# A first expert layer that computes only the chosen experts, block by block, in a four-layer kernel

## What is computed

```python
x = x + tanh(g_xattn[0]) * xattn0(layernorm(x), ...)          # long filter, stage A
x = x + tanh(g_ffn[0]) * ffn0(layernorm(x), ...)              # experts, stage B
x = x + tanh(g_xattn[1]) * xattn1(layernorm(x), ctx, ctx)     # attention, stage C
x = x + tanh(g_ffn[1]) * ffn1(layernorm(x), ...)              # shared matrices with adapters, stage D
# ffn0, E, K = 8, 2 ; F = 176 ; FS = 704
probs = softmax(x @ Wr)
routing_weights, selected = top_k(probs, K)
C = einsum('tk,tke->te', routing_weights, one_hot(selected, E))
expert_out = vmap(lambda wg, wu, wd: silu(x @ wg) * (x @ wu) @ wd)(Wg, Wu, Wd)
moe_out = einsum('te,eth->th', C, expert_out)
shared = sigmoid(x @ Wsg) * (silu(x @ Sg) * (x @ Su) @ Sd)
out = moe_out + shared
```

## Time and profile before

| | us |
|---|---|
| median of 3 runs | 888.54 |
| lowest and highest | 885.79 and 888.65 |
| the profiled execution | 884.61 |
| its span | 882.9 |
| stage A | 0 to 179.6 |
| stage B | 179.6 to 481.9 |
| stage C | 481.9 to about 618 |
| stage D | to the end |

### The profile page before, as it was taken

The page is one execution under the profiler, slowest core; times in us unless marked ns, Lnnn a source line. Parts: engine busy times, 40 slices in busy tenths (PEclk is TensorE's granted clock), DMA queues, the critical chain, the costliest instruction groups (busy, mean ns, idle before and its releaser), DMA issues.

```text
span 882.9 us, 13668 instructions
## 1 busy us (share of the span) xinstructions
PE 790.2 (90%) x4692; PEld 638.1 (72%) x4708; DVE 613.5 (69%) x1231; ACT 325.4 (37%) x521; POOL 163.9 (19%) x176
## 2 busy tenths in 40 slices
PE   3887879689999999999999899987789999999995
PEld 2565757578978888887887566655568787887884
DVE  5999999654465466446645888888377867778754
ACT  2120212033343342333233678765245335343221
POOL 1899989600000000000000112111000000000000
PEclk9999999799999999999999899997789999999997
DMA  7221212000000000000000121210101001001000
GB/s 274 73 81 56 71 48 66 18 1 1 1 1 0 0 0 0 0 0 27 25 0 15 40 85 56 86 48 1 49 0 49 1 25 49 1 25 49 24 1 24
DMA packets 21147, 30.24 MB, mean 34 GB/s; under 512 B 3760, under 2 KB 16112, under 8 KB 20464
## 3 DMA queue, kind: packets, MB, share of 16 engines
q1 hardware_dynamic: 21104, 29.69, 10.2%
HBM read 27.55 MB, written 2.13 MB: 34 GB/s over the span
## 4 chain that ended last, share of the span: by engine, by line
PE 67%; DVE 18%; issue 7%; POOL 3%; ACT 3%; DMA 1%; DVEq 0%; SPq 0%; POOLq 0%; ACTq 0%
PE bank L1630 23%; PE bank L1484 20%; PE bank L1497 11%; DVE small L1062 2%; PE bank L1551 2%; DVE A L868 2%; DVE A L857 2%; PE bank L1537 2%; POOL A L449 2%; DVE A L1072 2%; PE bank L1409 2%; ACT A L632 1%; PE bank L1411 1%; PE bank L1410 1%; PE bank L1562 1%
## 5 line engine op out<-in xcount | busy, mean ns | idle before, releaser
L1630 PE MATMUL bank<-R 128*128 128x512 f32 (+4 forms) x1104 | 225.9, 365 | 19.1 <-DVE A L1190 5.0
L1630 PEld LDWEIGHTS bank<-R 128*128 128x128 f32 (+2 forms) x1104 | 182.3, 188 | 60.1 <-issue 6.0
L1484 PE MATMUL bank<-R 128*128 128x512 f32 (+1 forms) x816 | 198.0, 392 | 1.9 <-issue 1.9
L1484 PEld LDWEIGHTS bank<-R 128*128 128x128 f32 (+1 forms) x816 | 146.7, 185 | 33.2 <-issue 2.1
L1009 DVE TENSOR_TENSOR A<-bank,A 128x512 f32<-128x512 f32 (+1 forms) x68 | 47.0, 691 | 119.9 <-PE bank L1484 119.9
L1497 PEld LDWEIGHTS bank<-R 128*128 128x128 f32 (+1 forms) x816 | 105.8, 190 | 10.8 <-issue 4.0
L574 ACT ACTIVATE A<-bank 128x512 f32<-128x512 f32 (+1 forms) x68 | 40.7, 599 | 194.6 <-PE bank L1484 194.6
L1497 PE MATMUL bank<-R 128*128 128x256 f32 (+1 forms) x816 | 109.4, 283 | 2.5 <-DVE R L1020 2.1
L1409 PE MATMUL bank<-A 128*128 128x256 f32 x128 | 45.4, 438 | 26.1 <-DVE A L857 17.6
L449 POOL TENSOR_TENSOR A<-A 128x256 f32<-128x256 f32 x64 | 64.3, 1004 | 12.4 <-DVE A L868 12.4
L1202 DVE TENSOR_TENSOR A<-bank,A 128x512 f32<-128x512 f32 (+1 forms) x48 | 32.9, 685 | 33.0 <-PE bank L1630 32.8
(11 more groups left out here) (166 smaller groups left out, 1105.2 us busy)
## 6 DMA issues: line engine op xcount, KB each, us to landing
A<-in_w SPq DMA_DIRECT2D x17, 384.0 KB, 3.1
A<-rows_d SPq DMA_DIRECT2D x4, 1024.0 KB, 4.7
A<-in_w SPq DMA_DIRECT2D x8, 480.0 KB, 3.5
A<-in_ctx_one SPq DMA_DIRECT2D x8, 272.0 KB, 3.5
A<-in_ctx_half SPq DMA_DIRECT2D x8, 256.0 KB, 3.1
A<-in_ctx_nat SPq DMA_DIRECT2D x4, 512.0 KB, 3.6
A<-in_ctx_t SPq DMA_DIRECT2D x128, 16.0 KB, 2.0
out<-X SPq DMA_DIRECT2D x4, 512.0 KB, 2.9
```

What stands on the lines that cost most here:

```text
L1484: mm = nc.tensor.matmul(dst[0:pr], wX[:, j, at + k * P:at + k * P + pr], mX[:, k], start=(n == 0), stop=(n == 5))
L1630: mm = nc.tensor.matmul(dst, a, m, start=start and n == 0, stop=stop and n == len(prods) - 1, skip_group_check=skip)
```

## The change

Stage B now computes the shared expert for all tokens, and the eight experts only for the rows that chose them.

- Routing gives every token two slots, one in each chosen expert's region of a table x_d in the chip's memory (18304 rows of 264 numbers: 256 of the normalised token and 8 weights). The rank of a token in its expert comes from matmuls with a triangle of ones (b_rank). Group 0 is routed as part 0, during stage A; the other twelve sequences are part 1, routed in one go beside the shared tiles of group 1.
- GpSimd scatters the rows: 32 indirect transfers of 128 rows, 8 for part 0 and 24 for part 1.
- A table of 39 blocks (NBLK, 32 full and up to 7 begun ones) says for each block where its 128 rows start and which expert it belongs to. SyncE, TensorE and VectorE load from it into registers (TENSOR_LOAD): one a block on SyncE, two on TensorE, one on VectorE.
- A block: SyncE loads 128 rows, TensorE turns them (2 matmuls), 6 matmuls of 352 columns give gate and up with tokens in the partitions, 2 turn the hidden part, 6 of 256 columns give down; ScalarE rounds twice and takes SiLU, VectorE subtracts twice, multiplies, and scales the result by the token's weight into yo; SyncE stores it to y_d. Four steps of different blocks are interleaved. Six row buffers (xb) and four result buffers (yo) are used in turn.
- GpSimd gathers: 32 indirect transfers with addition bring two rows of y_d back into X for each token.
- The order is: shared tiles of groups 0 and 1 (PRE = 2), the 39 blocks, shared tiles of groups 2 and 3. The last shared tile, 64 columns, now holds gate and up side by side, 6 matmuls in place of 12.
- The experts' weights are loaded (experts_in), rounded on ScalarE and subtracted on GpSimd in 10 chunks beside the first shared tiles. In stage A only the six shared tiles are split, 4 of them between heads; the inverse root there is one power on GpSimd (a_pow).
- Stage C takes over the statistics of groups 2 and 3 into its steps. Stage D packs its last tile in the same way (d_base_tail). Loops over groups are written out.

```diff
+NBLK = 2 * B + E - 1
...
+NCHUNK = 10
...
+SPLITS = {(0, 5): 2, (0, 10): 3, (1, 5): 4, (1, 10): 5}
...
+            for i in range(E - 1):
+                sp.dma_start(x_d[E * CAP + i * P:E * CAP + (i + 1) * P, :], zeros).then_inc(rows_zeroed, 16)
+            sp.wait_ge(table_ready, 1)
+            for i in range(E):
+                at = sp.value_load(tz[0:1, i:i + 1], min_val=0, max_val=E * CAP)
+                sp.dma_start(x_d[bass.ds(at, P), :], zeros).then_inc(rows_zeroed, 16)
+            sp.wait_ge(rows_zeroed, 16 * (2 * E - 1))
+            sp.wait_ge(rows_scattered, 16 * 2 * B)
+            def block_in(i):
+                if i < 6:
+                    if i < 4:
+                        sp.wait_ge(xsL_ready, NCHUNK)
+                else:
+                    sp.wait_ge(y_made, i - 5)
+                at = sp.value_load(trow[0:1, i:i + 1], min_val=0, max_val=X_ROWS - P)
+                sp.dma_start(xb[i % 6], x_d[bass.ds(at, P), :]).then_inc(blk_loaded[i % 6], 16)
+            def block_out(i):
+                sp.wait_ge(y_made, i + 1)
...
+            def a_pow(g):
+                pool.wait_ge(ve_ready, g + 1)
+                nc.gpsimd.tensor_tensor(rs[:], ve[:], mhalf, ALU.pow).then_inc(pow_ready, 1)
...
+                    if (g, h) in SPLITS:
+                        split_low(SPLITS[g, h])
...
+            def scatter(b):
+                for r in range(2):
+                    nc.gpsimd.indirect_dma_start(
+                        out=x_d[:, :], out_offset=bass.IndirectOffsetOnAxis(ap=slots[:, b, r:r + 1], axis=0),
+                        in_=row_of(b), in_offset=None).then_inc(rows_scattered, 16)
+            def gather(b, r):
+                nc.gpsimd.indirect_dma_start(
+                    out=X[:, b], out_offset=None, in_=y_d[:, :],
+                    in_offset=bass.IndirectOffsetOnAxis(ap=y_slots[:, b, r:r + 1], axis=0),
+                    compute_op=ALU.add).then_inc(gathered[r], 16)
...
+                pool.wait_ge(y_stored[i], 16 * ((NBLK - 1 - i) // 4 + 1))
+            pool.wait_ge(y_slots_ready, 2)
+            for g in range(G):
+                if g == PRE and PRE < G - 1:
+                    zero_keys()
+                pool.wait_ge(b_done, 1 + 2 * (g + 1))
+                for b in range(g * BG, (g + 1) * BG):
+                    gather(b, 0)
+                pool.wait_ge(gathered[0], 16 * BG * (g + 1))
+                for b in range(g * BG, (g + 1) * BG):
+                    gather(b, 1)
 
             def split_low1(g, r):
...
+            def blk_low_x(i):
+                dve.wait_ge(bxH_ready, i + 1)
+                nc.vector.tensor_tensor(bxL[:, i % 2], XT[i % 2][:, 0:D], bxH[:, i % 2].bitcast(F32), ALU.subtract
+                                        ).then_inc(bxL_ready, 1)
+            def blk_hidden(i):
+                dve.wait_ge(bsilu_ready, i + 1)
+                if i >= 2:
+                    dve.wait_ge(bh_turned, i - 1)
+                nc.vector.tensor_tensor(bh[:, i % 2, 0:EF], GU[i % 2][:, EF:2 * EF], bsilu[:, i % 2, 0:EF], ALU.mult
+                                        ).then_inc(bh_ready, 1)
+            def blk_low_h(i):
+                dve.wait_ge(bhH_ready, i + 1)
+                nc.vector.tensor_tensor(bhL[:, i % 2], HT[i % 2][:, 0:D], bhH[:, i % 2].bitcast(F32), ALU.subtract
+                                        ).then_inc(bhL_ready, 1)
+            def blk_out(i):
+                col = dve.value_load(tcol[0:1, i:i + 1], min_val=D, max_val=D + E - 1)
+                dve.wait_ge(bdown_ready, i + 1)
+                if i >= 4:
+                    dve.wait_ge(y_stored[i % 4], 16 * (i // 4))
+                nc.vector.tensor_scalar(yo[i % 4], DB[i % 2][:, 0:D], xb[i % 6][:, bass.ds(col, 1)], None, ALU.mult
+                                        ).then_inc(y_made, 1)
...
+            def blocks():
+                blk_low_x(0)
+                for s in range(NBLK + 2):
+                    if s + 1 < NBLK:
+                        blk_low_x(s + 1)
+                    if s < NBLK:
+                        blk_hidden(s)
+                    if s >= 2:
+                        blk_out(s - 2)
+                    if 1 <= s <= NBLK:
+                        blk_low_h(s - 1)
 
...
+                if g + 2 < G:
+                    dve.wait_ge(gathered[1], 16 * BG * (g + 3))
+                    norm = c_norm(BG * (g + 2), BG * (g + 3))
...
-                    pe.wait_ge(silu_ready, J0 * g + j - 1)
-                else:
-                    pe.wait_ge(h_ready, 1 + J0 * g)
-                for at, dst in ((0, G_[j % 2]), (2 * P, U_[j % 2])):
-                    if j >= 2 and at:
-                        pe.wait_ge(scaled_ready, J0 * g + j - 1)
-                    n = 0
...
+            def blk_gate_up(i):
+                at = pe.value_load(t16[0:1, i:i + 1], min_val=0, max_val=(E - 1) * RANK)
+                pe.wait_ge(bxL_ready, i + 1)
+                if i >= 2:
+                    pe.wait_ge(bh_ready, i - 1)
+                m = 0
+                for xX, wX in ((bxH, guH), (bxH, guL), (bxL, guH)):
+                    w = wX.rearrange("p (j a k c) -> p k a j c", j=EJ, a=2, k=DT)
+                    for k in range(DT):
+                        mm = nc.tensor.matmul(GU[i % 2][:, 0:2 * EF], xX[:, i % 2, k * P:(k + 1) * P],
+                                              w[:, k, :, :, bass.ds(at, RANK)], start=(m == 0), stop=(m == 5))
+                        m += 1
+                mm.then_inc(bgu_ready, 1)
...
+            def blk_down(i):
+                at = pe.value_load(t256[0:1, i:i + 1], min_val=0, max_val=(E - 1) * D)
+                pe.wait_ge(bhL_ready, i + 1)
+                if i >= 2:
+                    pe.wait_ge(y_made, i - 1)
+                m = 0
+                for hX, w0_, w1_ in ((bhH, dH0, dH1), (bhH, dL0, dL1), (bhL, dH0, dH1)):
+                    for rows, w in ((P, w0_), (EK, w1_)):
+                        a0 = 0 if w is w0_ else P
+                        mm = nc.tensor.matmul(DB[i % 2][:, 0:D], hX[0:rows, i % 2, a0:a0 + P],
+                                              w[0:rows, bass.ds(at, D)], start=(m == 0), stop=(m == 5))
+                        m += 1
+                mm.then_inc(bdown_ready, 1)
...
+            def blocks():
+                pe.wait_ge(table_ready, 1)
+                pe.wait_ge(h_ready, 1 + SJ * PRE)
+                pe.wait_ge(b_done, 1 + 2 * PRE)
+                blk_turn(0)
+                for s in range(NBLK + 1):
+                    if s + 1 < NBLK:
+                        blk_turn(s + 1)
+                    if s < NBLK:
+                        blk_gate_up(s)
+                    if s >= 2:
+                        blk_down(s - 2)
+                    if s >= 1:
+                        blk_turn_h(s - 1)
+                pe.wait_ge(bhL_ready, NBLK)
+                pe.wait_ge(bxL_ready, NBLK)
+                b_gate_up(SJ * PRE)
+                blk_down(NBLK - 1)
 
...
+            def d_base_tail(g):
+                j = SJ - 1
+                pe.wait_ge(tail_packed, 2)
+                dst = U_[j % 2]
+                three(dst, [(w1_tile(j, k * P, P), (xH[:, k], xL[:, k])) for k in range(DT)], stop=False, skip=True)
+                three(dst, [(w1_tile(j, 4 * P, P), (dzH[:, 0], dzL[:, 0]))], start=False, stop=False, skip=True)
+                return three(dst, [(w1_tile(j, 4 * P + TAIL, P), (dzH[:, 2], dzL[:, 2]))], start=False, skip=True)
...
+            for g in range(PRE):
+                b_group(g)
+                if g + 1 < PRE:
+                    b_gate_up(SJ * (g + 1))
+                    b_side(SJ * (g + 1))
+                b_down(SJ * g + SJ - 1)
+                if g + 1 < PRE:
+                    b_side_late(SJ * (g + 1))
+            blocks()
+            for g in range(PRE, G):
+                if g > PRE:
+                    b_gate_up(SJ * g)
+                b_group(g)
+                b_down(SJ * g + SJ - 1)
+            pe.wait_ge(h_ready, 1 + SJ * G)
...
```

940 lines of the change are left out of this document (638 added, 302 removed).

## The result

The changed kernel takes 946.0 us (median of 4 runs, 942.8 to 948.3) against 887.2 us for the kernel before on the same chip: a ratio of 1.066 with an interval of 1.062 to 1.070. It is slower; the forecast was 846 and its range ended at 895. The profiled execution took 942.8 us, its span is 941.1 (before: 884.6 and 882.9).

What follows compares the result with a forecast made beforehand. The prediction took TensorE, busy 90% of the span, to bound the kernel, with VectorE pacing part of stage A. From 884.6 us, -9 - 29.9 + 5 - 5.5 = -39.4 gave 845; it predicted 846, range 800 to 895.

Steps and rivals of the forecast that it cites:

- the ring: Stage B blocks: load of block i+5 issued only behind block i's store; 2T = 3.5 + 2.7, T = 3.1 us.
- T: Period of one block in stage B's loop; forecast 3.3 us, 39 blocks plus 4 for filling making 132.7 us.
- the rival of the prediction: Blocks: register loads stand in the open on TensorE, at 1.3 us each T = 4.7; 901 us, chance 0.13.
- the gap: Stage B ahead of the blocks: TensorE idle 31.3 us for 24 scatters, landings and first block; ends 17 and 50.
- The price of a down product: Blocks on TensorE: each 256-column down product takes 0.119 us, six of them within 2.11 us of work a block.
- The clock: Blocks: a granted clock of 0.77 at 73% busy lengthens 1.9 us of products; a reason for 3.3 over 3.1.
- The first two shared groups: Stage B ahead of the gap: 47.4 us of tiles, 60 with turnings, logits, edges and stalls; ends 55 and 72.
- The last two groups: Stage B behind the blocks: shared tiles with nothing beside them, 48.4 us with their end.
- Stage A: Before stage B: Newton steps and stalls beside GpSimd leave VectorE, routing adds 2 us; -9 us, ends -3 and -16.
- Stage C: Attention stage: takes over two groups' statistics, 4.5 us each on VectorE, half showing; +5 us, ends 0 and +9.
- The one on indirect transfers: Scatters and gathers: indirect transfers cost 2 us or more each, gap grows by 19; 879 us, chance 0.17.
- The faster one: Blocks run at TensorE's pace, register loads nearly free and landings short, T = 2.4; 811 us, chance 0.2.

Runs made afterwards that it cites:

- the first experiment: Changed kernel with each block's six down products issued as three of 128 rows, then three of 48, instead of alternating: 910.5 us, ratio 1.028.
- the ring and none: Changed kernel with each 48-row down product replaced by the 128-row one, leaving out part of the sum: 902.4 us, ratio 1.018.

## Experiments: what held the blocks

**Rows loaded one block sooner, on top of the order by rows.** Six row buffers were there; only the place in SyncE's queue held the load back.

```
-for i in range(4):
+for i in range(5):
     block_in(i)
 for i in range(NBLK):
-    if i + 4 < NBLK:
-        block_in(i + 4)
+    if i + 5 < NBLK:
+        block_in(i + 5)
     block_out(i)
```

> By rows as in the first experiment, and SyncE issues the load of block i+5 ahead of the store of block i, not behind it (five loads ahead of the loop, where there were four). Theory (with the row changes gone, the period of 3.4 to 3.6 us is the ring of store, load and landing that the prediction wrote down): TensorE's waits for a block's rows (35 us in the first experiment) go, the period at full clock falls to TensorE's own work and hand-overs, 2.8 to 3.0 us, and the clock stays over 0.9: 38 x (3.67 - 2.9) = 29 us less than 910.5, about 881 (875 to 888). Rival (the landing itself, or the register load ahead of the gate/up products, 0.41 us in the open, sets the period): 3.2 us or more, 893 to 910.

Measured: 876.2, T 2.77, 1.3% less than the kernel before (the interval ends at 0.994). By now it seemed that the ring mattered only once the changes of rows were gone, so the sooner load was also tried alone.

> The changed kernel with its alternating down products as they are, and only the row loads issued one block sooner. Theory (TensorE's own 3.56 us a block at full clock is later than the ring of loads, so the ring costs nothing here): 941 to 948, no change. Rival (part of the blocks' 4.31 us is the ring, through the half-clock stretches that its waits bring): 925 to 938.

Measured: 900.4. That theory fell: one line in SyncE's order is worth 46 us with every change of rows still there. The table by stretch:

```profile
300.00:350.00 50.00, 50.00 (x241) 36.83 (x241) 23.62 (x61) 14.65 (x45) 0.00 (x0) 1.00 0.27 79
350.00:395.00 45.00, 45.00 (x218) 33.03 (x217) 21.05 (x54) 12.70 (x39) 0.00 (x0) 1.00 0.27 81
```

TensorE is busy 50.0 of 50 with 241 matmuls, where the changed kernel was busy 47.1 with 176, and the clock is 1.00 instead of 0.80. The single periods are 3.33 at full clock (the 3.23 of the table has the three short ones in it): that is TensorE's own pace with six changes of rows.

**The ring shortened at its other end.** On TensorE the gate/up products of block s are put ahead of the turning of block s+1.

> The changed kernel, alternating rows and late loads as they are, with one pair of steps swapped on TensorE in the block loop: the gate/up products of block s stand ahead of the turning of block s+1, not behind it. Loading one block sooner took 46 us off (900) where no change was expected, so the old theory (TensorE's own 3.56 us are the limit) has fallen. New theory (the ring of store, load and landing holds the blocks; the turning that waits for the landing keeps the register steps and the six gate/up products behind it from starting, 1.7 us that stand in the ring): taken out of the ring, TensorE's own work of 3.33 us at full clock with the row changes becomes the limit and the clock stays up: 38 x (4.31 - 3.33) = 37 us less, 900 to 912. Rival (the sooner load helped for another reason, such as the spread of the DMA traffic over the period): 940 to 949.

Measured: 911.4, within the 900 to 912 of the theory. Most single periods are 3.32 to 3.39; T is 3.55, since some are longer, up to 4.86, with a mean clock of 0.95 over the blocks:

```profile
355.75 0.33 PE L2001 MATMUL bank<-ident,A 128*128 128x128 f32 x1
355.92 0.27 PE L2002 MATMUL bank<-ident,A 128*48 128x128 f32 x1
355.94 1.25 PE L1992 MATMUL bank<-R 128*128 x6
357.03 0.38 PE L1979 MATMUL bank<-ident,A 128*128 128x128 f32 x2
```

The loads are issued behind the stores as before, so the traffic is not it; the ring is.

**The ring in numbers.** In the changed kernel, from one store to the one two blocks on, 350.68 to 358.67, are 7.99 us, so 2T = 8.0 at full clock: 3.26 from the store to the turning (351.76 is its load, landed and turned at 353.94), 0.84 from the turning to the products, 1.29 to the down products, 1.87 for these, 0.73 to the next store. The 0.84 holds only 0.22 of turning. The rest are the register steps of the next products (a load of 0.30 us, arithmetic of 0.15, a check), which stand behind the wait in TensorE's program and so begin when it ends, the load at 353.93 like the turning itself: the [0.41 <-issue] above. One step earlier, where nothing was waited for, the same load ran at 349.5, beside the products before, and the gate/up products began 0.15 us behind the turning (350.22 and 350.37). The register steps of the down products make 1.29 of what is 1.08 with the loads one block sooner.

So the 4.51 from the fourth turning on are 3.33 of TensorE's own work, 0.67 that the ring adds (8.0/2), and 0.5 that are left, which goes with the stretches at half the clock: periods that fall into them take 5.6 to 6.0. The mean granted clock over the blocks was 0.80 with ring and changes of rows, 0.87 with the ring and two changes, 0.96 with the ring and none, 0.95 with all the changes and the products first, and 0.98 with all the changes and the loads sooner. So it takes both, waits for rows and stalls between products; how the two add up in the chip these runs do not settle.

**No register loads on TensorE.** All blocks take expert 1's weights at fixed addresses, in gate/up and down.

> The run with the early statistics (870), and TensorE loads no register in the blocks: all of them take expert 1's weights at fixed addresses. It prices the rival of the prediction in which the loads lie in the open. Theory (a load of 0.30 us runs ahead of the products of its step for the most part; between the last gate/up product and the first down product 0.1 to 0.3 us of it shows): 39 x 0.1 to 0.3 = 4 to 12 us less, 858 to 866. Rival (wholly hidden): 868 to 872. Rival of the prediction (0.65 us or more each in the open): 50 us less.

Measured: 857.6, 12.5 less than the 870.0 of the kernel with earlier statistics (below), with T 2.45 instead of 2.77: 0.32 us a block for two register loads and what belongs to them, a little over the 0.1 to 0.3 of the theory. It prices them where no rows are waited for; in the changed kernel the load of the gate/up products also stands in the ring, as above. From one block's products to the next's, 340.76 to 343.24:

```profile
340.76 1.24 PE L1991 MATMUL bank<-R 128*128 128x352 f32 x6
341.84 0.82 PE L2011 MATMUL bank<-R 128*128 128x256 f32 x4
...
343.24 1.24 PE L1991 MATMUL bank<-R 128*128 128x352 f32 x6
```

2.48 less two changes at 0.19 is 2.10; the forecast had 2.11 for the products and turnings alone. (No kernel was run that has neither.)

## Experiments: the shared groups around the blocks

**The first eight scatters behind the expert chunks.** They stand between chunk 1 and 2 on GpSimd, and ahead of the 11.78 us of idle at 211.11 ScalarE waits 8.19 us for a chunk's load, with the hidden tile's SiLU behind it.

> The eight scatters of the first four row groups are issued behind the ten expert chunks on GpSimd, not between chunk 1 and 2. Theory (the 12 us idle of TensorE before 211 in the first shared groups comes from the chunk loads that wait for GpSimd behind the scatters): the idle goes, the later scatters fit ahead of the second routing part, 8 to 13 us less, 946 -> 933 to 938. Rival (the chunk loads themselves, or SyncE's small transfers, end last anyway): 0 to 3 us less, 943 to 949.

Measured: 951.3, no gain, although the 11.78 us are gone: 3.79 are left there, and the longest wait in the two groups is 4.25. Tried again on the mended blocks:

> As the run before it, and the first eight scatters behind the expert chunks. Alone this gave nothing on the time (951 against 946) although the first turning of a block came 3.7 us sooner, because the blocks then ran at a lower clock. Theory (that came from the row changes, which are gone): 3 to 5 us less than the run before it, about 869. Rival (the lower clock in the blocks comes from the longer stretch at full clock ahead of them, whatever they do): no gain.

Measured: 873.3 against 870.0, no gain either. GpSimd's timeline tells why, with the scatters early (first row) and late:

```profile
249.42 1.31 POOL L626 DMA_INDIRECT x_d<-A  x1 [8.31 <-DVE A L1297]
```

```profile
251.35 0.96 POOL L626 DMA_INDIRECT x_d<-A  x1 [0.30 <-issue]
252.62 0.96 POOL L626 DMA_INDIRECT x_d<-A  x1 [0.30 <-issue]
```

Early, the ninth scatter waits for VectorE's slots, 78.2 us behind the first shared product (171.26); late, it has no wait for slots but stands behind the eight, at 76.6 (175.98). The eight cost 10 to 11 us wherever they stand on GpSimd. Something is gained: from the first shared product to the first turning of a block it is 112.1 us late, against 114.2 in the run that it is compared with; but that run's profile began its shared tiles 4.7 us sooner, with the same stage A, and a gain of 2 us does not show in times that spread by 6 to 9. My first reading of the missing gain, that the lower clock in the blocks (T 4.50) ate it, does not explain the second run, whose blocks are as fast as the others.

**The low parts of the experts' weights only cleared.** On the kernel with late scatters, GpSimd clears them and does not subtract, so they are left out.

> The run with early statistics and late scatters (873), with the ten subtractions on GpSimd that make the low parts of the experts' weights (L622, 2.4 us each) replaced by clearing the same memory, so the low parts are left out. It prices the expert chunks in the first two shared groups. Theory (GpSimd's subtractions stall VectorE's small steps by 2.2 us each, four or five times, and hold the next chunk's load): the stalls of 2.3 us on VectorE are gone, the first scatter of the second part comes 72 us or less behind the first gate/up product where it came 76.6, and the time is 3 to 7 us less, 866 to 870. Rival (the chain from the norms over the logits to the ranks sets it, whatever GpSimd does): 76 us, 871 to 876.

Measured: 863.0, 10 less and so below the 866 to 870 of the theory, the ninth scatter 70.6 us behind the first shared product instead of 76.6, the first turning 106.0 instead of 112.1. VectorE's stalls beside GpSimd are gone: three small steps had taken 2.42, 2.23 and 2.33 us (L1061, L1073, L1216), and now none does. One line of VectorE with its least, median and most in ns, first where GpSimd subtracts, then where it clears:

```profile
L1216 DVE TENSOR_TENSOR A<-A,ramp x2: 257/1294/2332, 239.0 to 243.1; 128x96 f32<-128x96 f32 x2
```

```profile
L1216 DVE TENSOR_TENSOR A<-A,ramp x2: 258/258/259, 233.3 to 235.3; 128x96 f32<-128x96 f32 x2
```

GpSimd itself also works 14 us less (0.9 us a chunk for 2.3), and its queue is what the ninth scatter stands in. But GpSimd is idle for ScalarE's rounding of the next chunk 52.5 us with the subtractions and 59.7 without, so it is one link of a chain (load, rounding, subtraction, buffer free), and no engine that works throughout. So with late scatters the chain of the chunks sets the length of these groups, and GpSimd's link is worth 6 us of it; the share of VectorE's stalls in these is not told apart.

**Statistics of the first group sooner.** VectorE's `c_norm(0, BG)` two tiles sooner, ScalarE's `c_norm_one` one.

> As the run before it, and VectorE's statistics of the first group for the attention (L1428) stand two tiles sooner, ScalarE's normalising (L815) one tile sooner; TensorE's turning of q stays where it was. Theory (the 8.6 us of TensorE idle ahead of the turning of q in the last shared group are this chain of 4.6 us of small steps and 2.1 us of normalising, put behind the last tile's work): the idle goes, 6 to 9 us less than the run before it, about 873. Rival (VectorE then waits two tiles sooner for the gathers, with the hidden tiles queued behind it): 0 to 3 us less, or more time.

Measured: 870.0 against 876.2; the intervals overlap (0.978 to 0.988, 0.980 to 0.994), so the times alone do not show a gain. The trace is plainer. The idle of 8.63 us ahead of the turning of q is now 2.91, and the last two groups take 58.5 us for 66.6:

```profile
451.49 1.97 PE L1966 MATMUL bank<-ident,A 128*128 128x128 f32 x8 [2.91 <-ACT A L737]
```

**Three shared groups ahead, one behind** (`PRE = 3`).

> The run with deeper loads (876), with three shared groups ahead of the blocks and one behind, where it has two and two. Theory (the 24 later scatters, 1.26 us each, hold the gap of 27.6 us, and a shared group beside them hides it; the gathers need about 22 us a group behind the blocks, and only one shared group of 24 us is left to hide them): the gap falls to under 10 us and the third group runs at full clock, -20 us; the last group's turning of q and the first scores wait for gathers, +5 to +15 us: 861 to 871. Rival (the gathers come late for the whole attention stage, since the 32 of the first two groups take 40 us): +20 to +40, 876 to 896.

Measured: 863.1, a ratio of 0.972 (0.969 to 0.975) to the kernel before: the best version here that computes everything. TensorE's timeline at both ends of the blocks:

```profile
290.93 0.66 PE L1979 MATMUL bank<-ident,A 128*128 128x128 f32 x2 [2.33 <-DMA A<-x_d]
...
440.95 1.97 PE L1966 MATMUL bank<-ident,A 128*128 128x128 f32 x8 [12.75 <-ACT A L737]
```

The third group lies wholly in the gap: the blocks start at 290.9, as they do with two groups ahead. What it buys is partly given back: the turning of q waits 12.75 us for the gathers, and stages C and D take 419.8 instead of the 402.7 of the kernel with two groups ahead (876.2).

## Why the prediction was wrong, step by step

- **The price of a down product failed.** "6 x 0.160 + 6 x 0.119 + 4 x 0.11 = 2.11 us" took the 0.119 of 256 columns from tiles whose products all have the same rows. The 0.160 was right (0.167), the turns were right, and 2.10 came out once the changes were taken off; but every one of the six products stands at a change of rows, 0.312 us. Four changes fewer take the period from 3.34 to 2.84 from the fourth turning on, 0.50 us and not 4 x 0.19 = 0.76: from the first gate/up product to the first down product it is now about 1.3 us where it was 1.08, since the register steps between them, which the changes had covered, now show.
- **The ring was the right mechanism, and its sizes failed.** "2T = load + 2.7" with a load of 3.5: the load was 3.26. For the turning I had 0.22 and it is 0.84, since the register steps stand behind its wait; for the products 0.96, and 1.29; for down 0.71, and 1.87; for the rest 0.8, and 0.73. 6.2 became 8.0. The text had all the pieces: it named the ring, said that "the rows of a block are fetched late" and that TensorE has two register loads a block, and then placed these beside the ring instead of in it.
- **The clock was seen and under-priced.** I allowed 0.2 us of T for it and for the register loads together, from a stretch at 0.77; it came at 0.80 and the period of 4.51 has 0.5 that nothing else accounts for. It came with the ring and the changes of rows together, and goes with either.
- **The first two shared groups failed by 29 us.** I named the right scene, a late chunk, SiLU behind it, TensorE behind that, and gave it under 3 us. The idle times above 0.5 us there sum to 21.4 (11.78, 1.95, 0.53, 2.09, 3.94, 1.08), and the clock falls to 0.68 in the stretch around the longest. Taking the longest away moved the start of the blocks, counted from the first shared product, by 2.4 us at most: the chain of the chunks with GpSimd's 23 us of subtractions and 10 of scatters holds it, or VectorE's routing, whichever ends later. How the rest of the 29 us divides was not measured.
- **The last two groups failed by 20 us.** "48.4 with their end" left out 6.7 us of statistics and normalising behind the last tile (8.63 of idle), of which 8.1 came back when they were put sooner (66.6 to 58.5), and a clock of 0.88 and lower (475 to 500 us, 0.84 after it); that the clock makes up the other 10 us is argued, not shown.
- **What held.** A scatter is issued every 1.26 us (1.2 forecast), and the gap is 27.6 (31.3), by luck in part: the ninth scatter comes 8.4 us ahead of the end of the second group, where 3.5 was forecast, and the 24 take a little longer. Stage A gained 4.7, inside its ends of -3 and -16; that varied from 171 to 176 us for the first shared product between kernels with the same stage A. Stage C, up to the first of stage D's three-part products, lost 7.3 (+5, ends 0 and 9), stage D gained 2.4 where I had 5.5. Neither of these stages' edits was tried alone.
- **The rivals.** The slower one (register loads in the open, T = 4.7, 901) is near in T and mostly wrong in cause: a load is 0.30 us and not 1.3, and two cost 0.32 us a block where nothing is waited for. It is right for the gate/up load where it stands behind a wait for rows: up to 0.69 us, in 13 of some 36 periods (295 to 455 us). The one on indirect transfers is refuted for scatters (every 1.26 us); the gathers, every 1.84, come near it, and what they cost was not tried. The faster one, T = 2.4, is near what the kernel could do: 2.77 was reached, and 2.45 without register loads. Of what the text said the profile would show, the gap came as written, the pace did not, and the waits ahead of the products were of both kinds it named, for rows and "issue", one behind the other.

## What to carry to other kernels

Before pricing a matmul by its columns, look whether its neighbour has the same count of rows; write products of one row count in a row. In a loop of transfers and work, put the whole ring on paper from the rows, register steps behind a waiting instruction included, and ask which engine's program order holds a step that its data would allow: two edits of order, worth 70 us together, turned a kernel 6.6% slower than the one before into one 1.3% faster. A busy share of 94 to 96% at a clock of 0.8 is not an engine at its limit.

## What the runs showed of the hardware

- A matmul of 256 columns that follows one of another row count (128 and 48, 128 and 64) takes 0.31 us from start to start where both its neighbours differ, 0.21 to 0.22 where one does, 0.12 where none does; about 0.19 us a change, at full clock.
- A register load from on-chip memory takes TensorE 0.30 us and 0.15 more of register arithmetic (L1984, below), about half of what the prediction took for a load. Beside products that keep TensorE busy long enough they cost nothing (the loads of rows sooner, all six changes of rows: 3.33 us with no idle time); without the changes 0.32 us a block show, and behind a wait all of it.
- While GpSimd subtracts 1024 columns, small steps of VectorE that take 0.17 to 0.26 us can take 2.2 to 2.4; with the same memory cleared instead, none did.
- An indirect transfer of 128 rows is issued in 0.96 us, every 1.26; one that adds to its target takes 1.54, every 1.84 (L626 and L632):

```profile
L1984 PEldq TENSOR_LOAD <-A x39: 296/302/496, 292.4 to 456.8; - x39
...
L626 POOL DMA_INDIRECT x_d<-A x32: 956/960/1610, 187.9 to 285.9; - x32
...
L632 POOL DMA_INDIRECT X<-y_d,A x32: 1531/1542/3104, 476.5 to 552.7; - x32
```
